# Cross-attention of a decoder layer: VectorE's order within a chunk, the bias on VectorE, other PSUM banks for the normed rows, another order of the first loads

## What is computed

```python
x = _layernorm(x + _L0_attn_ref(x, qkv_w, qkv_b, proj_w, proj_b))       # out = out @ proj_w + proj_b
x = _layernorm(x + _L0_xattn_ref(ctx_1024, x, Wq, Wk, Wv, Wo, bo, gx, bx, gl, bl))
x = _layernorm(x + _L0_ffn_ref(x, router_w, w1, b1, w2, b2))

def _L0_xattn_ref(x, latents, ...):             # x: the context, latents: the 4096 rows
    xn = layer_norm(x, gx, bx); ln = layer_norm(latents, gl, bl)
    q = (ln @ Wq) * SCALE;  k = xn @ Wk;  v = xn @ Wv                    # 8 heads of 64
    attn = softmax(einsum('bmhd,bnhd->bhmn', q, k))
    return einsum('bhmn,bnhd->bmhd', attn, v) @ Wo + bo
```

## Time and profile before

| what | us |
|---|---|
| median of 3 runs (lowest, highest) | 3881.74 (3879.18, 3888.47) |
| the profiled execution, its own time | 3886.65 |
| its span, first to last instruction | 3884.5 |
| of it: self-attention | 0 to 2205 |
| cross-attention, its head (to the first scores) | 2205 to 2303 |
| cross-attention, chunk 0 / chunks 1 to 6 / chunk 7 and end | 2303 / 2363 to 2771 / 2867 |
| experts | 2867 to 3884.5 |
| busy: PE, DVE, POOL, ACT (share of the span) | 90%, 66%, 54%, 45% |

### The profile page before, as it was taken

The page is one execution under the profiler, slowest core; times in us unless marked ns, Lnnn a source line. Parts: engine busy times, 40 slices in busy tenths (PEclk is TensorE's granted clock), DMA queues, the critical chain, the costliest instruction groups (busy, mean ns, idle before and its releaser), DMA issues. The chain is left out here.

```text
span 3884.5 us, 51792 instructions
## 1 busy us (share of the span) xinstructions
PE 3494.0 (90%) x18133; PEld 2290.6 (59%) x18134; DVE 2552.2 (66%) x4514; ACT 1735.6 (45%) x3066; POOL 2085.9 (54%) x1039
## 2 busy tenths in 40 slices
PE   7999999999999999999999578787859889999885
PEld 5455455454554554545543156766749778888774
DVE  6777777777777777777775156777634655556666
ACT  2455555555555555555555332232213433333342
POOL 1789898889898988888988600211110001100112
PEclk9999999999999999999998788998869899999998
DMA  6321312222213132222100211221122233323332
GB/s 216 102 54 59 94 51 87 68 63 83 74 56 104 47 91 69 63 83 68 56 23 4 88 61 44 79 79 55 44 106 81 97 105 109 103 90 104 120 115 97
DMA packets 190735, 309.76 MB, mean 80 GB/s; under 512 B 25609, under 2 KB 72329, under 8 KB 190490
## 3 DMA queue, kind: packets, MB, share of 16 engines
q1 hardware_dynamic: 164330, 238.58, 19.7%
q0 software_dynamic: 15072, 45.89, 3.4%
q10 hardware_dynamic: 11088, 22.02, 1.7%
...
## 5 line engine op out<-in xcount | busy, mean ns | idle before, releaser
L463 DVE TENSOR_REDUCE sa_part_max<-sa_mx 128x1 f32<-128x512 f32 x2048 | 1281.5, 679 | 542.4 <-PE sa_mx L574 538.3
L426 ACT ACTIVATE sa_prob<-sa_sc 128x512 f32<-128x512 f32 x2048 | 1121.8, 595 | 823.3 <-PE sa_sc L620 780.7
L247 POOL TENSOR_TENSOR sa_quad_sum<-sa_quad_sum,sa_prob 128x1024 f32<-128x1024 f32 x512 | 1208.8, 2397 | 7.3 <-ACT sa_prob L426 7.3
L574 PE MATMUL sa_mx<-sa_k_stack,sa_q_stack 96*128 96x512 f32 x2048 | 966.0, 474 | 27.8 <-DVE sa_part_max L463 15.9
L620 PE MATMUL sa_sc<-sa_q_stack,sa_k_stack 98*128 98x512 f32 x2048 | 865.4, 424 | 8.1 <-ACT sa_prob L426 8.1
L247 POOL TENSOR_TENSOR sa_quad_sum<-sa_prob 128x1024 f32<-128x1024 f32 x256 | 616.6, 2431 | 253.8 <-ACT sa_prob L426 253.8
L574 PEld LDWEIGHTS sa_mx<-sa_k_stack,sa_q_stack 96*128 96x128 f32 x2048 | 389.6, 190 | 377.9 <-issue 205.8
L620 PEld LDWEIGHTS sa_sc<-sa_q_stack,sa_k_stack 98*128 98x128 f32 x2048 | 388.9, 190 | 318.1 <-ACT sa_prob L426 273.4
L1809 PE MATMUL ex_h<-ex_xT,ex_w 128*128 128x384 f32 (+2 forms) x2688 | 469.0, 330 | 80.8 <-DVE ex_xT L1711 28.6
L1809 PEld LDWEIGHTS ex_h<-ex_xT,ex_w 128*128 128x128 f32 x2688 | 451.6, 196 | 105.9 <-issue 70.9
L589 PE MATMUL sa_pv<-sa_prob,sa_v 128*32 128x512 f32 x4096 | 501.7, 608 | 0.7 <-ACT sa_prob L426 0.7
...
...
## 6 DMA issues: line engine op xcount, KB each, us to landing
...
sa_xT<-xT SPq DMA_DIRECT2D x57, 1024.0 KB, 5.1
...
sa_prob<-in_x_dram ACTq DMA_DIRECT2D x8, 1024.0 KB, 7.2
```

The costliest lines, as they stand in the source:

```text
L247: pool.tensor_tensor(quad_sum[:, i % 2, heads, :], so_far, prob[:, k, heads, :], ALU.add).then_inc(quad_ready, 1)
L426: act.activation(prob[:, kt % 4, j, :], sc[n % 2][:, :], ACT.Exp, scale=SCALE).then_inc(prob_ready, 1)
L463: dve.reduce_max(part_max[:, q, j, k:k + 1], mx[n % 3][:, :], AX_X).then_inc(max_read, 1)
L574: pe.matmul(mx[n % 3][:, :], q_stack[0:QK, j, at:at + P], k_stack[0:QK, g // NQ % 2, j, k * BANK:(k + 1) * BANK], start=True, stop=True).t ...
```

## The change

- DVE: of `norm2(n)` only `variances` stays at the end of chunk n. Its shift and scalings move into chunk n+1, behind `highest` of tile 0.
- DVE: `low_a` moves ahead of `highest` of tile 2; `residual1` is done tile by tile between the `probabilities`; `place_tokens` moves behind `norm1`, between `low_p` of tiles 1 and 2.
- `add_bias` moves from POOL to DVE, as four instructions on 128 x 512: in the head (chunks 0 and 1), and for chunk n+2 between `low_p` of tiles 2 and 3 of chunk n.
- PE: `transpose_x1n` writes banks 6, 0, 2, 1 in place of 0, 1, 2, 3, so that only its last quarter waits for the last `low_p`.
- ACT: `high_a` stands ahead of the exponentials of tile 1, and `norm_y` behind `leave_x2T`, just ahead of `leave_p`.
- Head: the context has a semaphore of its own (`in_cin`), so norming it waits for its own load alone; the bias and the small vectors (now six loads on `in_c`) are waited for where they are used. ACT loads the projection's weights first and issues the other four matrices once they are in.
- The folding of `vw` (`values_wo`, `leave_vw`) moves from ahead of the first scores to behind them, in chunk 0.

```diff
         @block.sync
-            sp.dma_start(cin, a.ctx.rearrange("b m c -> m b c")).then_inc(in_c, 16)
+            sp.dma_start(cin, a.ctx.rearrange("b m c -> m b c")).then_inc(in_cin, 16)
...
         @block.gpsimd
-            pool.wait_ge(in_c, 7 * 16)
-            add_bias(0)
...
             for n in range(NCH):
                 if n + 1 < NCH:
-                    add_bias(n + 1)
+                    rstds(n + 1, 0)
                 if n >= 2:
                     send_rows(n - 2)
-                if n + 1 < NCH:
-                    rstds(n + 1, 0)
                 rstds(n, 1)
...
         @block.vector
-            dve.wait_ge(in_c, 7 * 16)
+            dve.wait_ge(in_cin, 16)
...
+            def add_bias(n):
+                dve.wait_ge(in_x, (n + 1) * 16)
+                for t in range(TQ):
+                    last = dve.tensor_tensor(xb[:, t, :], xb[:, t, :], pb[:, :], ALU.add)
+                last.then_inc(xb_ready, 1)
...
             dve.wait_ge(first_mm, CN_MM)
+            dve.wait_ge(in_c, 6 * 16)
...
             low_a(0, range(KC))
-            residual1(0)
+            add_bias(0)
+            residual1(0, range(TQ))
...
             leave_x1nT(0)
-            for h in range(XH):
...
-            low_vw(0)
+            add_bias(1)
             dve.wait_ge(qk_out, 16)
             for n in range(NCH):
                 more = n + 1 < NCH
                 highest(n, 0)
+                if n > 0:
+                    norm2(n - 1)
                 highest(n, 1)
-                if n >= 2:
-                    place_tokens(n - 2)
-                highest(n, 2)
                 if more:
                     low_a(n + 1, range(KC))
+                highest(n, 2)
                 probabilities(n, 0)
                 highest(n, 3)
-                for t in range(1, TQ):
-                    probabilities(n, t)
-                if n == PER_B:
-                    low_vw(1)
-                if more:
-                    residual1(n + 1)
+                probabilities(n, 1)
+                if n == 0:
+                    probabilities(n, 2)
+                    probabilities(n, 3)
+                    leave_vw()
+                    low_vw(0)
+                    residual1(n + 1, range(TQ))
+                else:
+                    if more:
+                        residual1(n + 1, (0,))
+                    probabilities(n, 2)
+                    if more:
+                        residual1(n + 1, (1,))
+                    probabilities(n, 3)
+                    if n == PER_B:
+                        low_vw(1)
+                    if more:
+                        residual1(n + 1, (2, 3))
                 low_p(n, 0)
                 low_p(n, 1)
                 if more:
                     norm1(n + 1)
+                if n >= 2:
+                    place_tokens(n - 2)
                 low_p(n, 2)
+                if n + 2 < NCH:
+                    add_bias(n + 2)
                 low_p(n, 3)
...
                 residual2(n, (2, 3))
-                norm2(n)
+                variances(n, 1)
+            norm2(NCH - 1)
...
         @block.scalar
             act.dma_start(wp_in[:, :, :], w_tiles(a.proj_w)).then_inc(in_wp, 16)
-            act.dma_start(wk_in[:, :, :], w_tiles(a.Wk)).then_inc(in_w, 16)
...
             act.wait_ge(in_wp, 16)
+            act.dma_start(wq_in, w_tiles(a.Wq)).then_inc(in_w, 16)
...
...
             for n in range(NCH):
                 more = n + 1 < NCH
                 exponentials(n, 0)
-                exponentials(n, 1)
                 if more:
                     high_a(n + 1)
-                exponentials(n, 2)
-                exponentials(n, 3)
-                if n > 0:
-                    norm_y(n - 1)
+                for t in range(1, TQ):
+                    exponentials(n, t)
+                if n == 0:
+                    leave_vw()
+                    high_vw(0)
                 if n == PER_B:
                     high_vw(1)
                 if n > 0:
                     leave_x2T(n - 1)
+                    norm_y(n - 1)
...
         @block.tensor
+                    elif k == 0:
+                        pe.wait_ge(x2T_ready, (n - 1) * KC)
                     else:
-                        pe.wait_ge(pT_ready, n * TQ)
+                        pe.wait_ge(pT_ready, n * TQ - (1 if k < 3 else 0))
                     for t in range(TQ):
-                        last = pe.transpose(bank[k][:, t * P:(t + 1) * P], x1n[:, t, k * P:(k + 1) * P], ident[:, :])
+                        last = pe.transpose(bank[X1N_BANK[k]][:, t * P:(t + 1) * P], x1n[:, t, k * P:(k + 1) * P], ident[:, :])
...
+            pe.wait_ge(in_c, 6 * 16)
             for k in range(KC):
                 last = pe.transpose(bank[4][:, k * E:(k + 1) * E], rw_rows[:, k * P:(k + 1) * P], ident[0:E, 0:E])
```

More of the change, by code:

```diff
@@ L1017, in shifts, with residual1 @@
                                          in1=rstd[:, which, which, :], op0=ALU.mult, op1=ALU.mult).then_inc(shift_ready, 1)
-            def residual1(n):
+            def residual1(n, ts):
                 dve.wait_ge(xb_ready, n + 1)
-                for t in range(TQ):
+                for t in ts:
                     dve.wait_ge(a_mm, n * TQ + t + 1)
@@ L1025, in residual1 @@
                     stats(0, t, x1[:, n % 2, t, :], LN_OF[n, 0] * TQ + t)
-                variances(n, 0)
+                if t == TQ - 1:
+                    variances(n, 0)
             def norm1(n):
@@ L1085, in norm2 @@
             def norm2(n):
-                variances(n, 1)
                 shifts(n, 1)
@@ L1145, in place_tokens, with leave_vw @@
                 assert done[0] == (n + 1) * ROUTE_STEPS
+            def leave_vw():
+                for h in range(XH):
+                    dve.wait_ge(first_mm, QK_MM + h * B + 2)
+                    if h >= 2:
+                        dve.wait_ge(vw_moved[(h * B + 1) % 4], 16 * moves_until(h - 2, 1))
+                    dve.tensor_copy(vw_rows[:, (h * B + 1) % 4, :], bank[4 + (h * B + 1) % 4][0:M, :]).then_inc(vw_left[1], 1)
             dve.wait_ge(first_mm, CN_MM)
+            dve.wait_ge(in_c, 6 * 16)
             for k in range(KC):
@@ L1312, in _ @@
             high_x1nT(0)
-            for h in range(XH):
-                act.wait_ge(first_mm, QK_MM + h * B + 1)
-                if h >= 2:
-                    act.wait_ge(vw_moved[h * B % 4], 16 * moves_until(h - 2, 0))
-                act.activation(vw_rows[:, h * B % 4, :], bank[4 + h * B % 4][0:M, :], ACT.Copy).then_inc(vw_left[0], 1)
             norm1(0)
-            high_vw(0)
             for n in range(NCH):
@@ L1453, in rank, with values_wo @@
                 pe.matmul(bank[7][:, P + TQ * E:P + 2 * TQ * E], ones[:, :], cols, start=True, stop=True).then_inc(rank_mm, 1)
+            def values_wo():
+                pe.wait_ge(r1_ready, TQ)
+                for h in range(XH):
+                    half = slice(h % 2 * XD, (h % 2 + 1) * XD)
+                    for b in range(B):
+                        if h >= 2:
+                            pe.wait_ge(vw_left[b], h - 1)
+                        pe.matmul(bank[4 + (h * B + b) % 4][0:M, :], vT[half, h // 2, b * M:(b + 1) * M], wo_in[half, h // 2, :],
+                                  start=True, stop=True).then_inc(first_mm, 1)
             pe.wait_ge(idr, 1)
@@ L1487, in _ @@
             transpose_x1n(0)
-            pe.wait_ge(r1_ready, TQ)
-            for h in range(XH):
-                half = slice(h % 2 * XD, (h % 2 + 1) * XD)
-                for b in range(B):
-                    if h >= 2:
-                        pe.wait_ge(vw_left[b], h - 1)
-                    pe.matmul(bank[4 + (h * B + b) % 4][0:M, :], vT[half, h // 2, b * M:(b + 1) * M], wo_in[half, h // 2, :],
-                              start=True, stop=True).then_inc(first_mm, 1)
             pe.wait_ge(made, MADE)
@@ L1500, in _ @@
                 scores(n)
+                if n == 0:
+                    values_wo()
                 for t in range(TQ):
```

24 lines of the change are left out of this document (12 added, 12 removed).

## The result

The changed kernel takes **3849.41 us** (median of 4 runs, 3843.24 to 3854.22) against 3881.28 for the kernel before, taken beside it (4 runs): a ratio of 0.9914, 95% interval 0.9894 to 0.9934. That is 32 us faster where 87 were forecast, and outside the range (3766 to 3828). The profiled execution took 3851.77, its span 3849.8.

What follows compares the result with a forecast made beforehand. PE's waits between engines bound it, neither PE nor VectorE being full. 36.3 + 10.9 + 23.2 + 4.5 - 5.4 - 2 = 67.5, + 12.2 + 0 + 7 = 86.7; 3886.65 profiled became 3800.0, median 3795; range 3766 to 3828.

Steps and rivals of the forecast that it cites:

- The step that failed: VectorE's queue behind `outputs` of tile 0: moved `place_tokens` and bias end as tile 3's probabilities come, costed at nothing.
- The seam: Between chunks: `highest` of tile 0 comes before the shift, so the wait inside `scores` and its slow half go, 47.2 us.
- 36.3, 10.9 and 23.2: Gains in us, chunks 1 to 6: wait inside `scores`; its slow half; waits ahead of `project` and `transpose_x2`.
- The bias on VectorE: `add_bias` takes 2.5 us on VectorE; its wait for the `xb` load costs 2 in chunk 2 (bounds 0 and 11.2).
- The slower rival: `add_bias` waits for `xb` and blocks VectorE; decides from a landing 14.5 us late; 3891 at 16 late; chance 0.04.
- `norm_y` ahead of `leave_p`: On ACT it delays `low_p` of tile 0, a new PE wait of 0.8 to 0.9: -5.4 us in six chunks.
- The banks: New banks for `transpose_x1n` gain nothing: the 11.2 us wait moves to `outputs` of tile 2, waiting for `residual2`.
- The slow clock elsewhere: Chunks 1 and 5 lost about 9 us together to a lower clock; half, 4.5, comes back (bounds 0 and 9).
- The head: Before chunk 0: the context's norm runs beside the loads, so `project` starts 12.2 us earlier (bounds 9 and 17).
- Chunk 7: The 5.63 wait for `norm_y`, 2.1 in `scores` and its slow half go: 7 us gained (bounds 3 and 10).
- The clock stays high: Rival: the first `outputs` of each chunk also leaves half clock, and all 9 us elsewhere return: 3781; chance 0.15.
- VectorE becomes the bound: Rival: VectorE's covers of 1.3 to 1.8 us fail in each chunk and waits return one step later: 3851; chance 0.12.

Runs made afterwards that it cites:

- e2: The changed kernel with `place_tokens` moved mid-chunk, between `residual1` of tile 1 and the probabilities of tile 3: 3795.9 us, ratio 0.9774.
- e1: The changed kernel with `place_tokens` back in its old slot, between `highest` of tiles 1 and 2: 3814.2 us, ratio 0.9809.
- e5: The changed kernel with PE doing `route_logits` behind `outputs` of tile 0, VectorE's order untouched: 3826.1 us, ratio 0.9858.
- e4: The kernel before with only `norm2` moved behind `highest` of the next chunk's tile 0, `variances` staying at the chunk's end: 3862.6 us, ratio 0.9933.
- e8: e2 with the bias of chunks 2 to 7 on GpSimd again: 3820.7 us, ratio 0.9822.
- after: The changed kernel itself, with the whole change: 3849.4 us, ratio 0.9914.
- e7: e2 with ScalarE's `norm_y` ahead of `leave_x2T` again: 3803.5 us, ratio 0.9769.
- e6: e2 with `transpose_x1n` on the old banks 0 to 3 and with the old waits: 3795.3 us, ratio 0.9755.

## Why the prediction was wrong, step by step

- **The step that failed** is "the queue of VectorE is `norm1`, `place_tokens` (2447.82 to 2450.87, 3.05; it stands now in a gap that had 5.5 in chunk 2), `low_p` 2, the bias, `low_p` 3. They end at S + 43 to 44, as tile 3's probabilities come, so I cost them at nothing". The cover named there was VectorE's own: the gap in which it does the work. Who waits for the result was not asked. PE comes to its wait on `route` ahead of the logits at S + 27.6, while VectorE reads the ranks only at S + 35.4 (chunk 2). It cost 40.8 of waiting and 16.7 of half-speed logits in chunks 2 to 6 (38.5 against e2's 21.8), and 5.1 in chunk 7: 62.6. Without it the sum would be 34.9 + 62.6 = 97, above the 87 that were forecast, since the waits put at 5.4 (`norm_y`) and 2 (the bias) hardly showed behind it (0.5 and nothing) and the slow clock gave back more than the 4.5. The three runs that removed it one way or another (e1, e2, e5) gained 22 to 54 us; e2, the best of them, pays 10.2 of new waits for `ca_pT` for it.
- **Luck.** That e2's 3793.6 meets the forecast of 3795 does not show its terms to be right, and e2 is another kernel than the one forecast. Its six chunks last 67.7 less than before where 67.5 were forecast, but PE's busy time in them fell by 20.0 (15.4 forecast: 10.9 + 4.5) and its idle time by 47.7 (52.1 forecast). The two misses cancel.
- **The seam** was right: no wait between the halves of `scores`, both full speed (13.80 together; 14.1 forecast), the shift 0.15. e4 adds what the prediction's sum hides: the terms 36.3, 10.9 and 23.2 are not separate prices of separate edits. The move of `highest` alone gains only 26, since GpSimd's bias goes on holding the shift; e8 shows the same from the other side.
- **The bias on VectorE**: 2.49 measured, 2.5 taken. Its wait for the load was put at 2 in chunk 2. In the changed kernel none shows; in e2 it is 5.4: VectorE asks at S + 40.0, as forecast (39.7), and the load lands 14.3 after its issue, where a wait of 2 meant some 10. In the other chunks of e2 VectorE waited 0.2 for `xb` in all. The slower rival needed 14.5 in each chunk and did not come.
- **`norm_y` ahead of `leave_p`**: 5.4 forecast, 0.5 in after (chunk 1 alone; elsewhere it lies under the 8.07). e7 shows the two places traded for each other.
- **The banks**: nothing forecast, nothing found (e6); 1.59 ahead of `outputs` of tile 2 took the place of the 11.2, as written.
- **The slow clock elsewhere**: 4.5 of 9 given back in the forecast. In e2 chunks 1 and 5 last 54.5 and 54.4, no longer than chunk 6 (54.6), so all of it came back there.
- **The head**: 15.0 against 12.2, chunk 0 -3.9 against 0 (bounds 4 either way): 11.1 together. The wait for the store of `qk` in chunk 0 came as written, 3.63 on PE where 4 was put. **Chunk 7**: 7 forecast, 1.7 measured, 6.8 without its 5.13; 11.0 in e2, where its logits take 3.80 and took 6.84 before.
- **The rivals.** "The clock stays high" did not come: `outputs` of tile 0 took 5.06 to 5.88 in e2, and before 5.27 to 6.04 in five of the six chunks (3.73 in chunk 4). "VectorE becomes the bound" gave 3851, close to the measured time and for the wrong reason: e5 keeps VectorE's queue and is faster, and VectorE is busy 46.9 of 65.7 in chunk 2.
- The list of what would prove it wrong held one sign that came true (chunks over 58 us) but did not name `route_logits`: the walk counted its time within PE's 17.9 and did not ask what it waits for.
